# First attention of a four-stage kernel: VectorE's small steps moved ahead of the row maxima, statistics split in parts, two idle banks used for the first batches, and one all-engine barrier left out

## The chip, the cores and the metric

The kernel runs on one core of a Trainium2 chip. The metric is the device time of one execution in microseconds (us), lower is better. The kernel before took 1908.39 us (median of 3 runs, 1903.99 to 1915.61). The profile below is of another execution, which took 1909.73 us with a span of 1907.9 us.

## The reference

The input is x, 16 batches x 256 rows x 256 (4096 rows in all), and a context of the same shape. Four stages follow each other, each adding to x:

```
x = x + xattn0(layernorm(x), ctx)      # the stage that is changed
x = x + ffn0(layernorm(x))             # 8 experts, top 2
x = x + xattn1(layernorm(x), ctx)
x = x + ffn1(layernorm(x))

def xattn0(q, kv, Wq, Wkv, Wc):        # per batch: 256 queries, 256 context rows
    qp = q @ Wq.T
    idx = argmax(qp @ kv.T, axis=-1)   # best context row of each query
    mk, mv = split(kv[idx] @ Wkv.T)    # 16 + 16 columns
    logits = heads(qp) @ mk.T / 4      # 16 heads of 16 columns, 256 x 256 each
    return merge(softmax(logits) @ mv) @ Wc.T
```

## The kernel before

Everything is written as five instruction streams, one for each engine (TensorE, VectorE, ScalarE, GpSimd, and SyncE, which issues most DMAs). Streams meet only through semaphores, and each stream runs strictly in the order written. `Waits.wait_ge` issues a wait once and drops those already passed.

**First attention** (`pe_l0`, `dve_l0`, `act_l0`, `pool_l0`, `sp_l0`). The work is cut into 128 units u (batch u//8, two heads each) and runs over slots i = 0 to 147; g = i//8 is the batch that is scored, r = i%8 the place in it. In slot i TensorE computes the scores of unit i (`scores`, L426), VectorE takes their row maxima (`maxima`, L578, two reductions of 128x512). Fourteen slots later (LAG) TensorE computes the transposed scores with the maxima subtracted (`scores_turned`, L438), ScalarE takes the exponential (`weights`, L673), and every second slot TensorE multiplies by the values (`values`, L450) and ScalarE takes them out (`values_out`, L679). Scores of units rotate over three banks: those of slot u+1 need the first reduction of slot u to be done.

The other steps of a batch hang on a value of r:

- Entry of batch g+2, all in bank MB: r=1 `turn_x` (L477), r=2 `x_out` (L707, ScalarE), r=3 `queries` (L485), r=4 `queries_high` (L713, ScalarE) and `queries_low` (L595, VectorE), r=7 `matches` (L497); then at r=0 of the next batch `best` (L602, L606: the argmax on VectorE) and `memories` (L777: GpSimd gathers the chosen context rows).
- Keys of batch g+1: r=5 `turn_keys` (L505) and `context` of g+2 (L460), r=6 `context_out` (L693, L695) and `keys_high` (L720) on ScalarE, `keys_low` (L613) on VectorE. `matches` at r=7 waits for `keys_low`, since both use MB.
- Exit of batch g-3, all in bank MA: r=3 and r=5 `turn_values` (L512), r=4 and r=6 `divide` (L619, L621, VectorE), r=7 `turn_packed` (L519), r=0 `packed_out` (L725, ScalarE), r=1 `result` (L526), r=2 `result_add` (L627, VectorE), r=3 `stats_out` (mean, variance and a first guess of 1/sqrt, L118 to L133).
- `stats_x` at r=5 of batches 0, 4 and 8: the same statistics for 8 row tiles of x at once, L118 x8 to L133. Newton's steps for 1/sqrt run on GpSimd (`newton_pool`, 14 small operations).

In a slot VectorE did `maxima` first and then what hangs on r; ScalarE did `weights` first. Slots 128 to 147 have no scores; TensorE runs `kv_tile` there (L359, L365: keys and values of the second attention) and VectorE copies the result (L402), again first in its slot. The last batches leave at slots 139 to 147.

**Prologue.** The entries of batches 0 and 1 run before slot 0, both in MB, so one after the other: `best(1)` comes ahead of slot 0. VectorE starts when three transfers have landed (4 row tiles, a weight and the identity).

**Barrier.** `phase_end` (L163 to L167) follows on each engine: a drain, an increment of one semaphore, and a wait until all five have arrived. Then come `pe_route` and its fellows, where VectorE normalises all rows (L159 into XNF) and TensorE transposes them (L953), computes router logits (L962) and one `kv_tile` per step.

Of the kernel before, what the change touches and what calls it, by code (L numbers as in the profile page):

```python
# [56 lines left out]
def build(nc, A, OUT):  # L57
# [57 lines left out]
    def stats_dve(e, w, k, t0, n, mv, r, src, twice=False):  # L115
        v, u, r = LTMP[:, k % 2 * 2, 0:n], LTMP[:, k % 2 * 2 + 1, 0:n], r[:, t0:t0 + n]
        for t in range(t0, t0 + n):
            i = e.bn_stats(ST[:, t, :], src(t))  # L118
        i.then_inc(s_st, 1)
# [15 lines left out]
    def newton_pool(e, w, k, t0, n, r):  # L135
# [24 lines left out]


    s_end = sem("phase_end")

    def phase_end(e, w, n):
        e.drain().then_inc(s_end, 1)
        w.wait_ge(s_end, 5 * n)
# [98 lines left out]
    d_cst, d_w0_w1, d_ws_wr_wc1 = sem("d_cst"), sem("d_w0_w1"), sem("d_ws_wr_wc1")  # L265
    d_x_wf2_out = [sem(f"d_x_wf2_out{i}") for i in range(4)]
    d_ct = [sem(f"d_ct{i}") for i in range(2)]
    d_qw, d_nm, d_x0_wkv_id = sem("d_qw"), sem("d_nm"), sem("d_x0_wkv_id")
# [5 lines left out]
    s_mh, s_wo, s_spl, s_ms = sem("keys0"), sem("outmm0"), sem("ctxsplit"), sem("memsets")  # L274
# [22 lines left out]
    use_a = {}  # L297
    use_b = {n: x for x, n in enumerate((("kv", 0), ("kv", 1), ("xt", 0), ("q", 0), ("am", 0), ("xt", 1), ("q", 1), ("am", 1)))}
    stat0, split_at, nsplit = {"first": 0, ("ln", 0): 1}, {0: 0, 1: 2}, 4
    for i in range(SLOTS0):  # L300
# [4 lines left out]
        for at, n, b in ((1, "xt", g + 2), (3, "q", g + 2), (5, "kv", g + 2), (7, "am", g + 2)):  # L305
            if r == at and is_batch(b) and (n, b) not in use_b:
                use_b[n, b] = len(use_b)
        if i in STAT_AT:
            stat0["o", STAT_AT[i]] = len(stat0)
        if r == 5 and g % 4 == 0 and g < 12:  # L310
            stat0["ln", g // 4 + 1] = len(stat0)
# [106 lines left out]
    def pe_l0(e, w):  # L418
# [35 lines left out]
        def context(b):  # L454
            w.wait_ge(d_x0_wkv_id, 48)
            w.wait_ge(d_ct[b % 2], 16 * (b // 2 + 1))
            w.wait_ge(s_mb, use_b["kv", b])
            for jt in range(2):
                for cc in range(2):
                    i = e.matmul(MB[:, 256 + jt * 32:288 + jt * 32], CT[b % 2][:, cc, jt * 128:jt * 128 + 128], WKV[:, cc, :],  # L460
                                 start=(cc == 0), stop=(cc == 1))
# [8 lines left out]
        def turn_x(b):  # L470
            w.wait_ge(d_x0_wkv_id, 48)
            w.wait_ge(s_xn, b + 1)
            w.wait_ge(s_mb, use_b["xt", b])
            w.wait_ge(s_mh, 3 if b == 2 else 0)
            for cc in range(2):
                for lt in range(2):
                    i = e.transpose(MB[:, cc * 256 + lt * 128:cc * 256 + lt * 128 + 128], XN[:, lt, cc * 128:cc * 128 + 128], ident)  # L477
            i.then_inc(s_xt, 1)

        def queries(b):  # L480
            w.wait_ge(d_w0_w1, 16)
            w.wait_ge(s_mb, use_b["q", b])
            for ec in range(2):
                for cc in range(2):
                    i = e.matmul(MB[:, ec * 256:ec * 256 + 256], WQ[:, cc, ec * 128:ec * 128 + 128], XNT[:, cc, :],  # L485
# [3 lines left out]
        def matches(b):  # L489
            q, c = (QH, QL), [CHL[b % 2][j][:, :].rearrange("p (a b) -> p a b", a=2) for j in range(2)]  # L490
            w.wait_ge(s_spl, split_at[b] + 2)
            w.wait_ge(s_mb, use_b["am", b])
# [1813 lines left out]
```

## Time and profile before

| what | value |
|---|---|
| runs | 1903.99, 1908.39, 1915.61 us |
| profiled execution | 1909.73 us, span 1907.9 us |
| TensorE busy | 1720.9 us, 90% |
| VectorE busy | 1284.1 us, 67% |
| ScalarE busy | 1136.5 us, 60% |
| GpSimd busy | 822.8 us, 43% |
| mean granted TensorE clock | 0.947 |
| first attention with its prologue | 0 to about 445 us |

A line of the page's table of slices shows the busy share of an engine in tenths for each fortieth of the span; the clock line shows the granted TensorE clock in the same way. TensorE's busy time is modelled, since matmuls are pipelined; its idle gaps are therefore more telling than its share.

### The profile page before, as it was taken

The page shows a single profiled execution, that of the slowest core. Times are in us where ns is not written, and L with a number is a line of the kernel's source. Part 1 is how long each engine was busy: PE and PEld are TensorE (multiplying, and loading weights), DVE is VectorE, ACT ScalarE, POOL GpSimd, SP SyncE. Part 2 cuts the span into 40 slices and gives each one's busy share as a digit, 9 for nine tenths or more (in the row PEclk, how much of TensorE's full clock was granted, in tenths as well). Part 3 has the DMA queues.
Part 4 walks back from the last instruction along what each step waited for, and adds up shares of the span by engine and source line. Part 5 has one row for each costly group of instructions (what it writes and reads, how often), then busy time and mean ns, then how long its engine had stood idle before and what let it go on. Part 6 is the DMA issues. An engine that isn't in the chain of part 4 may idle for free.

```text
span 1907.9 us, 41070 instructions
## 1 busy us (share of the span) xinstructions
PE 1720.9 (90%) x15760; PEld 1451.1 (76%) x15760; DVE 1284.1 (67%) x2756; ACT 1136.5 (60%) x2882; POOL 822.8 (43%) x1306
## 2 busy tenths in 40 slices
PE   5789898887999999999999879999999999987648
PEld 3566666666989999999999768788888888866523
DVE  3677887643532888888888386777777777677321
ACT  1356565532336777777777477777777777744210
POOL 3233432111011333333331387888888887654000
PEclk8789999998999999999999999999999999999766
DMA  6754465234786666666676722222222321112699
GB/s 180 202 124 104 107 123 116 61 116 166 263 281 215 246 246 246 243 232 234 244 245 239 234 73 86 71 62 68 90 68 62 92 65 57 43 48 91 233 366 328
DMA packets 140163, 303.81 MB, mean 159 GB/s; under 512 B 14080, under 2 KB 82944, under 8 KB 124736
## 3 DMA queue, kind: packets, MB, share of 16 engines
q1 hardware_dynamic: 116032, 188.68, 32.3%
q0 software_dynamic: 19584, 108.31, 16.8%
q10 hardware_dynamic: 4352, 4.20, 0.6%
q8 instruction: 125, 2.05, 0.4%
q14 instruction: 70, 0.57, 0.1%
HBM read 210.44 MB, written 90.44 MB: 158 GB/s over the span
## 4 chain that ended last, share of the span: by engine, by line
PE 71%; DVE 12%; DMA 5%; issue 5%; POOL 4%; ACT 2%; SPq 1%; POOLq 0%; DVEq 0%; ACTq 0%
PE ps L1230 11%; PE ps L1216 11%; PE ps L1812 5%; PE ps L359 5%; PE ps L223 4%; PE ps L1843 4%; PE ps L1798 4%; PE ps L1832 4%; PE ps L365 3%; DVE NM L578 2%; PE ps L426 2%; DMA rp_scratch<-RP 2%; PE ps L497 2%; PE ps L526 2%; POOL P L213 2%
## 5 line engine op out<-in xcount | busy, mean ns | idle before, releaser
L200 ACT ACTIVATE P<-ps,NM 128x256 f32<-128x256 f32 x512 | 236.2, 481 | 127.5 <-DVE NM L189 127.5
L213 POOL TENSOR_TENSOR P<-P,RS 128x1024 f32<-128x1024 f32 x128 | 242.9, 1903 | 73.7 <-DVE RS L207 73.3
L1216 PE MATMUL ps<-XRP,W1P 128*128 128x256 f32 x1872 | 226.8, 281 | 3.3 <-DVE W1P L1299 3.3
L1216 PEld LDWEIGHTS ps<-XRP,W1P 128*128 128x128 f32 x1872 | 220.1, 190 | 3.6 <-DVE W1P L1299 3.6
L1230 PE MATMUL ps<-W2P,HP 128*128 128x256 f32 x1872 | 221.5, 277 | 0.0
L673 ACT ACTIVATE PT<-ps 128x512 f32<-128x512 f32 x256 | 140.7, 611 | 132.5 <-PE ps L438 132.5
L1230 PEld LDWEIGHTS ps<-W2P,HP 128*128 128x128 f32 x1872 | 218.0, 188 | 0.0
L578 DVE TENSOR_REDUCE NM<-ps 128x2 f32<-128x512 f32 x256 | 164.3, 684 | 64.1 <-PE ps L426 63.9
L189 DVE TENSOR_REDUCE NM<-ps 128x2 f32<-128x512 f32 x256 | 164.6, 684 | 5.6 <-PE ps L1798 4.1
L1150 POOL DMA_INDIRECT WE<-in_we,WIX x39 | 44.2, 1135 | 278.5 <-DVE W1P L1299 209.2
L1259 ACT ACTIVATE HF<-ps,WE 128x256 f32<-128x256 f32 x312 | 129.0, 465 | 43.3 <-PE ps L1216 43.3
L1931 DVE CAST OT<-ps 128x256 fp32r<-128x256 f32 x128 | 54.3, 424 | 141.1 <-PE ps L1812 140.2
L1798 PEld LDWEIGHTS ps<-K,Q 64*128 64x128 f32 x1536 | 100.8, 189 | 59.5 <-issue 42.4
L230 ACT ACTIVATE PT<-ps 128x512 f32<-128x512 f32 x256 | 140.7, 616 | 1.5 <-PE ps L223 1.5
L1812 PE MATMUL ps<-PT,V 128*64 128x256 f32 x1024 | 138.9, 392 | 1.1 <-DVE OT L1933 1.1
L223 PE MATMUL ps<-CST,P 128*128 128x128 f32 x1024 | 133.9, 274 | 3.1 <-ACT PT L230 3.1
L1798 PE MATMUL ps<-K,Q 64*128 64x256 f32 x1536 | 127.3, 299 | 10.3 <-DVE Q L1925 5.4
L1250 ACT ACTIVATE W2P<-WE 128x512 fp32r<-128x512 f32 x156 | 97.3, 624 | 53.9 <-PE ps L1230 53.9
L1146 POOL DMA_INDIRECT XR<-xn_scratch,RIX x78 | 79.4, 1018 | 102.2 <-PE ps L1192 48.1
L223 PEld LDWEIGHTS ps<-CST,P 128*128 128x128 f32 x1024 | 115.1, 141 | 4.6 <-issue 3.9
L1316 DVE TENSOR_TENSOR HP<-HF,HP 128x512 fp32r<-128x512 f32 x156 | 108.0, 692 | 13.2 <-ACT HP L1266 5.7
L1832 PE MATMUL ps<-XNP,W1Q 128*128 128x256 f32 x768 | 110.9, 295 | 4.4 <-POOL XNP L2105 4.4
(219 smaller groups left out, 3710.2 us busy)
## 6 DMA issues: line engine op xcount, KB each, us to landing
KS<-k_scratch SPq DMA_DIRECT2D x64, 256.0 KB, 3.1
V<-v_scratch SPq DMA_DIRECT2D x16, 1024.0 KB, 6.3
rp_scratch<-RP SPq DMA_DIRECT2D x16, 1024.0 KB, 8.8
R<-rp_scratch SPq DMA_DIRECT2D x16, 1024.0 KB, 13.9
k_scratch<-KVM SPq DMA_DIRECT2D x52, 256.0 KB, 4.2
QS<-q_scratch SPq DMA_DIRECT2D x96, 128.0 KB, 4.8
v_scratch<-KVM SPq DMA_DIRECT2D x40, 256.0 KB, 3.0
ys_scratch<-YS SPq DMA_DIRECT2D x39, 256.0 KB, 8.2
```

Of the source, the lines that this page charges most:

```text
L189: e.tensor_reduce(self.NM[:, u % 4, 2 * x:2 * x + 2], PS[SB[n % 3]][:, :].rearrange("p (h j) -> p h j", h=2), AX.X, ALU.max, negate=True). ...
L200: i = e.activation(self.P[u % 4][:, c, :], PS[SB[n % 3]][:, y * 256:y * 256 + 256], ACT.Exp, bias=self.NM[:, u % 4, c:c + 1], accum_out=se ...
L213: e.tensor_tensor(p, p, self.RS[:, u % 4, :].unsqueeze(2).to_broadcast([128, 4, 256]), ALU.mult).then_inc(self.s_pn, 1)
L223: i = e.transpose(PS[TB[h]][:, c0:c0 + 128], self.P[u % 4][:, c, jt * 128:jt * 128 + 128], ident)
L230: e.activation(self.PT[u % 4][h][:, :], PS[TB[h]][:, :], ACT.Copy).then_inc(self.s_tv, 1)
L578: e.tensor_reduce(NM0[b % 2][:, :, 8 * h + p], PS[SB[(2 * u + h) % 3]][:, :].rearrange("p (l j) -> p l j", l=2), AX.X, ALU.max, negate=Tru ...
L673: e.activation(PT0[u % 4][h][:, :], PS[TB[h]][:, :], ACT.Exp).then_inc(s_ex0, 1)
L1216: m = e.matmul(PS[p][:, hh * 256:hh * 256 + 256], W1P[i % 2][wi][:, cc * 1024 + hc * 128:cc * 1024 + hc * 128 + 128], XRP[i % 2][xi][:, cc ...
L1230: m = e.matmul(PS[4 + k][:, s * 256:s * 256 + 256], HP[k][hi][:, hc, s * 128:s * 128 + 128], W2P[k][wi][:, hc * 256:hc * 256 + 256], start ...
L1798: m = e.matmul(PS[SB[(2 * u + h) % 3]][:, lt * 256:lt * 256 + 256], Q1[i][64 * h:64 * h + 64, p, lt * 128:lt * 128 + 128], K1[j][64 * h:64 ...
L1812: m = e.matmul(PS[OB][64 * h:64 * h + 64, 0:256], V1[b % 2][:, jt, (2 * p + h) * 64:(2 * p + h) * 64 + 64], a1.PT[u % 4][h][:, jt * 256:jt ...
L1832: m = e.matmul(QB[:, j * 256:j * 256 + 256], W1Q[wi][:, cc, c0:c0 + 128], XNP[b % 2][xi][:, cc, :], start=(cc == 0 and x == 0), stop=(cc = ...
```

## The change

Six edits, all but one in the first attention:

1. On VectorE `divide` and `result_add` stand ahead of the slot's `maxima` (or copy), `keys_low` behind them.
2. On ScalarE `x_out`, `queries_high`, `context_out`, `keys_high` and `packed_out` stand ahead of the slot's `weights`.
3. `stats_x` is cut into four parts, at r = 1, 3, 5, 7 of the same batches; the first three take 2 tiles each, the last 2 tiles and the rest of the work.
4. In the prologue batch 1 uses bank MA (`entry`), its context and that of batch 0 the banks PS[3] and PS[4] (`context_bank`). `best(1)` moves into slot 0. The order is written anew.
5. The first transfer brings 2 row tiles and not 4, with a semaphore of its own; Newton's steps for them run on VectorE (`newton`, the old `newton_pool` under another name).
6. `phase_end` is gone. SyncE waits for the last `result` before it loads the router's weights.

```diff
+        def stats_x(c, part):
             w.wait_ge(d_x_wf2_out[c], 16)
-            stats_dve(e, w, stat0["ln", c], 8 * c, 8, MV, RSTD, lambda t: X[:, t, :])
+            if part < 3:
+                stats_rows(e, 8 * c + 2 * part, 2, lambda t: X[:, t, :])
+            else:
+                stats_dve(e, w, stat0["ln", c], 8 * c, 8, MV, RSTD, lambda t: X[:, t, :], before=6)
...
-        w.wait_ge(d_x0_wkv_id, 48)
-        stats_dve(e, w, stat0["first"], 0, 4, MV, RSTD, lambda t: X[:, t, :])
+        w.wait_ge(d_x0, 16)
+        stats_dve(e, w, stat0["first"], 0, 2, MV, RSTD, lambda t: X[:, t, :])
+        newton(e, w, stat0["first"], 0, 2, RSTD)
         norms(0)
         w.wait_ge(d_x_wf2_out[0], 16)
-        stats_dve(e, w, stat0["ln", 0], 4, 4, MV, RSTD, lambda t: X[:, t, :])
+        stats_dve(e, w, stat0["ln", 0], 2, 6, MV, RSTD, lambda t: X[:, t, :])
+        queries_low(0)
         norms(1)
-        queries_low(0)
         best(0)
         queries_low(1)
-        best(1)
         keys_low(0)
-        w.wait_ge(d_cst, 32)
+        w.wait_ge(d_cst_wc, 32)
         for i in range(SLOTS0):
             g, r = i // 8, i % 8
-            if i < U:
-                maxima(i)
-            else:
-                tile_out_dve(e, w, i - U)
-            if r == 6 and is_batch(g + 1):
-                keys_low(g + 1)
             if i in DIV0:
                 divide(DIV0[i], 0)
             if i in DIV1:
                 divide(DIV1[i], 1)
             if i in ADD_AT:
                 result_add(ADD_AT[i])
+            if i < U:
+                maxima(i)
+            else:
+                tile_out_dve(e, w, i - U)
             if i in STAT_AT:
                 stats_out(STAT_AT[i])
-            if r == 0 and g and is_batch(g + 1):
+            if r == 0 and is_batch(g + 1):
                 best(g + 1)
             elif r == 4 and is_batch(g + 2):
                 queries_low(g + 2)
-            elif r == 5 and g % 4 == 0 and g < 12:
-                stats_x(g // 4 + 1)
+            elif r == 6 and is_batch(g + 1):
+                keys_low(g + 1)
+            elif r % 2 and g % 4 == 0 and g < 12:
+                stats_x(g // 4 + 1, r // 2)
...
         context_out(0)
-        context_out(1)
         x_out(0)
         queries_high(0)
+        context_out(1)
         x_out(1)
...
-            if 0 <= i - LAG < U:
-                weights(i - LAG)
             if i in PACK_AT:
                 packed_out(PACK_AT[i])
-            if r == 1 and is_batch(g - 1):
-                max_out(g - 1)
-            elif r == 2 and is_batch(g + 2):
+            if r == 2 and is_batch(g + 2):
                 x_out(g + 2)
-            elif r == 3 and is_batch(g + 3):
-                norms(g + 3)
             elif r == 4 and is_batch(g + 2):
                 queries_high(g + 2)
             elif r == 6 and is_batch(g + 1):
                 if is_batch(g + 2):
                     context_out(g + 2)
                 keys_high(g + 1)
+            if 0 <= i - LAG < U:
+                weights(i - LAG)
+            if r == 1 and is_batch(g - 1):
+                max_out(g - 1)
+            elif r == 3 and is_batch(g + 3):
+                norms(g + 3)
...
-            phase_end(e, w, 1)
```

(The last line stands on all five engines.) VectorE's stream in slots r = 4 to 7 of one batch was this; L578 are the maxima (two for each slot), L619 and L621 a division, L595 `queries_low`, L613 `keys_low`:

```order
L578 TENSOR_REDUCE NM_85<-ps 128x2 x2
L619 RECIPROCAL RS_97<-ps 128x16
L621 TENSOR_TENSOR ON<-ps,RS_97 128x256
L595 SCALAR_TENSOR_TENSOR QL<-ps,QH 128x512
L578 TENSOR_REDUCE NM_85<-ps 128x2 x4
L613 TENSOR_TENSOR MKS_78<-ps,MKS_78 16x256 x2
L619 RECIPROCAL RS_97<-ps 128x16
L621 TENSOR_TENSOR ON<-ps,RS_97 128x256
L578 TENSOR_REDUCE NM_85<-ps 128x2 x2
```

Now it is this (L592 the maxima, L636 and L638 the division, L612 `queries_low`, L630 `keys_low`):

```order
L636 RECIPROCAL RS_97<-ps 128x16
L638 TENSOR_TENSOR ON<-ps,RS_97 128x256
L592 TENSOR_REDUCE NM_85<-ps 128x2 x2
L612 SCALAR_TENSOR_TENSOR QL<-ps,QH 128x512
L592 TENSOR_REDUCE NM_85<-ps 128x2 x2
L636 RECIPROCAL RS_97<-ps 128x16
L638 TENSOR_TENSOR ON<-ps,RS_97 128x256
L592 TENSOR_REDUCE NM_85<-ps 128x2 x2
L630 TENSOR_TENSOR MKS_78<-ps,MKS_78 16x256 x2
L592 TENSOR_REDUCE NM_85<-ps 128x2 x2
```

Both divisions stand ahead of their slot's maxima, and the second one is no longer behind `keys_low`.

ScalarE's stream in slot r = 6 of a batch was this; PT are the exponentials, CKV `context_out`, MKS `keys_high`, OT `values_out`:

```order
L673 ACTIVATE PT_87<-ps 128x512
L673 ACTIVATE PT_88<-ps 128x512
L693 ACTIVATE CKV<-ps 128x128 x2
L695 ACTIVATE CKV<-ps 128x2x16
L720 ACTIVATE MKS_76<-ps,CST 128x256
L679 ACTIVATE OT_96<-ps 128x256
```

Now it is this:

```order
L710 ACTIVATE CKV<-ps 128x128 x2
L712 ACTIVATE CKV<-ps 128x2x16
L737 ACTIVATE MKS_76<-ps,CST 128x256
L690 ACTIVATE PT_87<-ps 128x512
L690 ACTIVATE PT_88<-ps 128x512
L696 ACTIVATE OT_96<-ps 128x256
```

The four operations on context and keys stand ahead of the two exponentials. Behind the change VectorE's slots 0 to 3 of batch 0 read so (L592 the maxima, L619 and L623 `best(1)`, L117 parts of the statistics of x):

```order
L592 TENSOR_REDUCE NM_84<-ps 128x2 x2
L619 MAX MX<-ps 128x8 x2
L623 MAX_INDEX MI<-MX,ps 128x8 x2
L592 TENSOR_REDUCE NM_84<-ps 128x2 x2
L117 BN_STATS ST<-X 128x6 x2
L592 TENSOR_REDUCE NM_84<-ps 128x2 x4
L117 BN_STATS ST<-X 128x6 x2
```

The argmax of batch 1 and the first two parts of the statistics lie between maxima that stood in a row before.

## Rows read from the trace of the kernel before

**Rows 1.** Stretches of the core's time; columns: length, busy us (count) of engines, clock, DMA

```profile
core 0: us, PE busy (x) PEld busy (x) DVE busy (x) ACT busy (x) POOL busy (x), PEclk, DMA share, GB/s
...
178.67:199.19 20.52, 18.29 (x186) 13.28 (x185) 16.42 (x39) 12.93 (x30) 8.41 (x21) 1.00 0.62 126
...
219.70:243.77 24.07, 19.65 (x186) 14.57 (x185) 20.08 (x58) 13.04 (x30) 11.21 (x35) 0.93 0.46 102
...
284.80:306.75 21.95, 19.72 (x186) 14.14 (x185) 16.26 (x39) 13.14 (x30) 6.58 (x19) 0.92 0.54 113
```

**Rows 2.** What TensorE waited for, 36 to 375 us: total, times, longest

```profile
PE ps L519 <- DVE ON L621: 22.4, 12, 2.0
PE ps L426 <- DVE NM L578: 15.4, 12, 3.5
```

**Rows 3.** A regular batch in order of time: start, busy us, what, [idle before]

```profile
178.50 0.98 PE L460 MATMUL ps<-WKV,CT 128*128 128x32 f32 x8
...
179.94 1.29 DVE L578 TENSOR_REDUCE NM<-ps 128x2 f32<-128x512 f32 x2 [0.64 <-PE ps L426]
...
180.19 1.08 ACT L673 ACTIVATE PT<-ps 128x512 f32<-128x512 f32 x2 [1.55 <-PE ps L438]
...
181.55 0.60 ACT L720 ACTIVATE MKS<-ps,CST 128x256 fp32r<-128x256 f32 x1
...
182.18 0.88 DVE L613 TENSOR_TENSOR MKS<-ps,MKS 16x256 fp32r<-16x256 f32 x2 [0.95 <-ACT MKS L720]
...
183.86 0.66 PE L519 MATMUL ps<-CST,ON 128*128 128x128 f32 x4 [2.03 <-DVE ON L621]
...
188.29 2.00 PE L526 MATMUL ps<-WC,ONT 128*128 128x256 f32 x8
...
192.50 0.68 DVE L627 TENSOR_TENSOR X<-X,ps 128x512 f32<-128x512 f32 x1
...
196.11 1.29 DVE L578 TENSOR_REDUCE NM<-ps 128x2 f32<-128x512 f32 x2
...
197.22 0.50 PE L426 MATMUL ps<-MKS,QS 48*128 48x256 f32 x4
```

**Rows 4.** The statistics of 8 tiles in batch 0, order of time

```profile
49.17 2.70 DVE L118 BATCH_NORM_STATS2 ST<-X 128x6 f32<-128x256 f32 x8
...
53.82 0.79 PE L426 MATMUL ps<-MKS,QS 48*128 48x256 f32 x4 [3.49 <-DVE NM L578]
```

**Rows 5.** A stretch of 2 us, columns as in rows 1

```profile
292.00:294.00 2.00, 2.00 (x18) 1.32 (x19) 0.76 (x2) 0.33 (x1) 0.00 (x0) 0.50 0.00 1
```

**Rows 6.** Who waited for whom, 350 to 447 us: total, times, longest

```profile
PE ps L519 <- DVE ON L621: 4.4, 3, 1.6
...
PE ps L512 <- DVE ON L621: 3.3, 3, 1.4
...
PE ps L512 <- DVE X L627: 1.5, 1, 1.5
```

**Rows 7.** The end of the stage and the barrier, order of time

```profile
439.04 0.17 DVE L133 TENSOR_SCALAR RSTD<-LTMP 128x2 int32<-128x2 int32 x1
...
445.71 6.55 DVE L159 TENSOR_SCALAR XNF<-X,MV,RSTD 128x256 f32<-128x256 f32 x20 [6.50 <-POOLq L165]
...
446.59 1.09 PE L953 MATMUL ps<-CST,XNF 128*128 128x128 f32 x4 [10.39 <-DVE XNF L159]
```

**Rows 8.** The prologue and first slots in order of time; last, L834's DMA landing

```profile
11.81 0.74 DVE L159 TENSOR_SCALAR XNa<-X,MV,RSTD 128x256 f32<-128x256 f32 x2 [3.40 <-POOL RSTD L146]
...
23.99 1.16 POOL L777 DMA_INDIRECT MVK<-ckv_scratch,MI  x1 [3.25 <-DVE MI L606]
...
31.64 0.83 SPq L831 DMA_DIRECT2D ctx_scratch<-CHL  x2
...
34.70 0.74 SPq L834 DMA_DIRECT2D X<-in_x  x1
...
40.19 1.29 DVE L578 TENSOR_REDUCE NM<-ps 128x2 f32<-128x512 f32 x2 [0.48 <-PE ps L426]
...
DMA to landing us min/median/max: 9.8/9.8/9.8
```

More of the change, by code:

```diff
@@ L113, in build, with stats_rows, stats_dve @@
     s_st, s_nw = sem("ln_guess"), sem("ln_newton")
-    def stats_dve(e, w, k, t0, n, mv, r, src, twice=False):
-        v, u, r = LTMP[:, k % 2 * 2, 0:n], LTMP[:, k % 2 * 2 + 1, 0:n], r[:, t0:t0 + n]
+    def stats_rows(e, t0, n, src):
         for t in range(t0, t0 + n):
             i = e.bn_stats(ST[:, t, :], src(t))
-        i.then_inc(s_st, 1)
+        return i
+    def stats_dve(e, w, k, t0, n, mv, r, src, twice=False, before=0):
+        v, u, r = LTMP[:, k % 2 * 2, 0:n], LTMP[:, k % 2 * 2 + 1, 0:n], r[:, t0:t0 + n]
+        stats_rows(e, t0 + before, n - before, src).then_inc(s_st, 1)
         w.wait_ge(s_st, 5 * k + 1)
@@ L295, in is_batch, with entry, entry_free, entry_done @@
         return 0 <= b < 16
-    use_a = {}
-    use_b = {n: x for x, n in enumerate((("kv", 0), ("kv", 1), ("xt", 0), ("q", 0), ("am", 0), ("xt", 1), ("q", 1), ("am", 1)))}
+    def entry(b):
+        return MA if b == 1 else MB
+    def entry_free(w, n, b):
+        if b == 1:
+            w.wait_ge(s_ma, use_a[n, 1])
+        else:
+            w.wait_ge(s_mb, use_b[n, b])
+    def entry_done(w, n, b):
+        if b == 1:
+            w.wait_ge(s_ma, use_a[n, 1] + 1)
+        else:
+            w.wait_ge(s_mb, use_b[n, b] + 1)
+    def context_bank(b):
+        return PS[TB[b]] if b < 2 else MB
+    use_a = {("xt", 1): 0, ("q", 1): 1, ("am", 1): 2}
+    use_b = {n: x for x, n in enumerate((("xt", 0), ("q", 0), ("am", 0)))}
     stat0, split_at, nsplit = {"first": 0, ("ln", 0): 1}, {0: 0, 1: 2}, 4
@@ L305, in build @@
         for at, n, b in ((1, "xt", g + 2), (3, "q", g + 2), (5, "kv", g + 2), (7, "am", g + 2)):
-            if r == at and is_batch(b) and (n, b) not in use_b:
+            if r == at and is_batch(b):
                 use_b[n, b] = len(use_b)
@@ L309, in build @@
             stat0["o", STAT_AT[i]] = len(stat0)
-        if r == 5 and g % 4 == 0 and g < 12:
+        if r == 7 and g % 4 == 0 and g < 12:
             stat0["ln", g // 4 + 1] = len(stat0)
@@ L530, in pe_l0 @@
         context(0)
-        context(1)
         turn_x(0)
         queries(0)
+        context(1)
         matches(0)
@@ L536, in pe_l0 @@
         queries(1)
+        turn_keys(0)
         matches(1)
-        turn_keys(0)
         for i in range(SLOTS0):
@@ L581, in norms @@
         def norms(b):
-            w.wait_ge(s_nw, newton_done(stat0["first"]))
+            w.wait_ge(s_nw, newton_done(stat0["ln", 0] if b else stat0["first"]))
             w.wait_ge(s_xt, b)
@@ L778, in memories @@
                                      in_offset=bass.IndirectOffsetOnAxis(ap=MI[:, lt, 0:1], axis=0)).then_inc(d_gk[b % 2], 16)
-        e.memset(CKV[:, :, :], 0.0).then_inc(s_ms, 1)
-        w.wait_ge(s_ms, 1)
-        e.memset(CKV[:, :, 144:145], 1.0).then_inc(s_ms, 1)
-        newton_pool(e, w, stat0["first"], 0, 4, RSTD)
+        e.memset(CKV[:, :, :], 0.0).then_inc(s_ms_ck, 1)
+        w.wait_ge(s_ms_ck, 1)
+        e.memset(CKV[:, :, 144:145], 1.0).then_inc(s_ms_ck, 1)
         split(0)
-        newton_pool(e, w, stat0["ln", 0], 4, 4, RSTD)
+        newton(e, w, stat0["ln", 0], 2, 6, RSTD)
         split(1)
```

109 lines of the change are left out of this document (53 added, 56 removed).

## The prediction

> **What bounds the kernel now.** I read the page first: TensorE is busy 90% of the span, so a gain must come from its gaps. Then the stretches between one batch's `context` and the next. A regular batch of the first attention takes 20.52 us, of which TensorE works 18.29 [rows 1], so 2.23 us are a gap; VectorE works 16.42 and ScalarE 12.93. Third, the list of who waited for whom: nearly all of the gap is one wait, `turn_packed` (L519) for the second division, 22.4 us in 12 waits [rows 2]. The timeline shows how it arises [rows 3]: the context matmuls end at 179.48 (178.50 + 0.98), yet ScalarE first does two exponentials (180.19), then CKV, and only at 181.55 the keys (L720); VectorE stands 0.95 us for them, does `keys_low` (182.18 to 183.06) and the division, and TensorE starts L519 at 183.86 after 2.03 us of nothing. The division's own input had long been there; it stood behind `keys_low` only by order. Two more gaps belong to this change. In three batches VectorE does the statistics of 8 tiles in one piece and TensorE waits 3.49 us for maxima [rows 4]; such a batch takes 24.07 us [rows 1]. And at the end of the stage TensorE waits 10.39 us from its last tile to L953 [rows 7].
>
> **The clock in these gaps.** After the same L519 gap two of the regular batches ran matmuls at a granted clock of 0.50 [rows 5], the lower of the two levels (1.2 GHz), and took 21.95 us [rows 1] (the next one alike) where their neighbours took 20.5. The engine had done nothing for 2.03 us just before the clock fell.
>
> **The change part by part.** The sum is made against the profiled execution, 1909.73 us (span 1907.9 and 1.8 around it), which lies 1.3 us above the median of the runs.
>
> *Divisions first, keys first.* In slot r=6 ScalarE can now start CKV at 179.5, not at 181.16; CKV and keys took 0.99 us together, so the keys stand at 180.5 instead of 182.15. VectorE does the division in the 0.64 us in which it stood before the maxima of 179.94 [rows 3]; maxima end near 181.3, `keys_low` near 182.2. L519 finds its input, `matches` waits for nothing more. The 22.4 us go. What is late next: the two exponentials begin at 180.5 instead of 180.19 and end near 181.6, while TensorE wants their banks at 181.33: 0.27 us per batch. The first division of a batch now stands between the statistics and the maxima of 196.11 and pushes them 0.5 us (the division takes 0.64; the addition, also moved, gives part back); TensorE's next scores come 0.74 us after a start of maxima wherever the trace has them waiting, so 197.35 against 197.22: 0.13 us. Thirteen batches x 0.40 = 5.2. Net **-17.2**. Bounds: -22.4 if neither is seen, and -6 if handing over between the engines costs a full 0.7 + 0.53 us once per batch. The addition (L627) ahead of the maxima costs nothing as long as L526, which ends at 190.29, is done before VectorE would start on its own, and that is near 190.5; the maxima before and after it were 0.8 us apart. `packed_out`, `x_out` and `queries_high` fall in gaps of ScalarE, which works 12.93 of 20.52 us [rows 1]; cover gone, each would cost the 0.60 us that such an operation takes (L720 in [rows 3]).
>
> *The clock dips behind those gaps.* Two batches gave 1.43 and 1.54, and the last scored batch, where after an idle 1.61 us the matmuls of 353 to 360 us ran at half clock, about 3. If the gaps go, so do these: up to -6, at least 0; I take **-5**. The Trainium skill, TensorE: Matmul & The Clock Gate, Part 1, says that activity releases the throttle and idling brings it back; by it the dips vanish with the idle stretches. This trace agrees in direction (clock 0.50 only behind a gap), but nine of the twelve L519 gaps brought no dip, so I don't take the rule as a switch.
>
> *Statistics in parts.* VectorE's chain through such a batch gets no shorter: from slot 0 to slot 10 I add up maxima, best, addition, statistics, divisions and the 4.3 us of parts to 25.7 us with the two handovers, against 23.2 for TensorE's. So these batches become bound by VectorE and exceed a regular one by 2.5 us and not by 3.55 (24.07 - 20.52). With the half-clock matmuls behind the long gap **-3** for batches 4 and 8 (0 to -6).
>
> *Prologue.* VectorE starts after one transfer of half the size and does Newton's steps itself, some 14 steps of 0.2 us; I put the first normalisation at 8.2 instead of 11.81 [rows 8] and, the rest of the chain being the same matmuls and outputs, the gather of batch 0 at 19.9 instead of 23.99. Batch 1's entry lies beside it in bank MA. Scores could start 6 us earlier. But SyncE waits for that gather (31.64) before it stores the split context, and only behind that, at 34.70, it asks for the next 8 row tiles, which land 9.8 us later, at 44.5 [rows 8]. Statistics needed them in slot 5 (49.17 [rows 4]); the first part now needs them in slot 1. Moved up by 4.1 us they land at 40.4, VectorE stands there with the maxima of slot 2 behind it, and these start near 41.1, where they start at 40.19 now. So the prologue's gain is all given back, with `best(1)` hidden in that wait. What is left is the hole of 3.49 us in slot 5, now spread: **-2.4** (bounds +1 and -8, the latter if the rows land as soon as they are wanted). In batches 1 and 2 `matches` waited about 1 us for `keys_low`, which now comes sooner: **-1.5**.
>
> *Tail, slots 128 to 147.* TensorE waits there for divisions and an addition that stand behind a copy which itself needs TensorE's tile of that slot: 4.4 - 1.6 (the one at 352 us is counted above) + 3.3 + 1.5 = 7.6 us [rows 6]. Ahead of the copy they run beside the tile. **-7**.
>
> *Barrier.* VectorE's last statistic ends at 439.2 and its first XNF starts at 445.71 [rows 7]: 6.5 us. Nothing in `dve_route` needs the other engines at once: the first Newton results are hundreds of us old, the last are needed only by the last of 32 normalisations, 20 of which take 6.55 us [rows 7]. The last copy and addition change places, 0.6 more. **-7** (bounds -4, if the loss of cover shows in a bank or a DMA, and -9 with a warmer clock at L953).
>
> *Beyond 447 us* nothing is changed. TensorE is bound there by itself and starts that much earlier; one wait for stores near 530 us moves along. I price it at nothing; cover gone, it is a few us.
>
> Sum: -17.2 - 5 - 3 - 2.4 - 1.5 - 7 - 7 = -43.1, so 1909.7 - 43.1 = **1866.6 us**.
>
> **The rivals.**
>
> *VectorE becomes the bound.* With 16.42 us of work and a dozen waits in 18.6 it has 12% left. If maxima late by half a us make TensorE wait in several slots, a batch takes 19.5: 11 us less gain, and small gaps keep some dips (5 us more): 1882. For it: 15.4 us of waits for maxima already [rows 2]. Against it: the tight slots (even for VectorE, odd for TensorE) alternate.
>
> *First in line is the wrong place (slower).* A division or addition at the head holds the maxima if its input is late. If the three moved steps each expose the matmuls they wait for (L526 2.0, L512 0.66 twice) and their own time (0.68 + 2 x 0.64), 5.3 us per batch come in for 2.0 that go: 13 x 3.3 = 43 us more, the dips stay, and with 21 us from elsewhere the time is 1909.7 + 43 - 21 = 1932. It decides when L526 ends later than VectorE finishes slot 1; the rows have 0.2 us to spare there before VectorE idles, and 1.0 before it costs anything. The same page of the Trainium skill (Architectural detail) calls ScalarE's and VectorE's queues strict FIFO; that rule speaks against putting waiting steps first, and by it alone the time would be this rival's. The row agrees with it: VectorE stood 0.95 us for keys with a ready division behind.
>
> *The rows are there in time.* If the tiles of x land 5 us sooner than I put it, the prologue keeps its gain: 1866.6 - 5.5 = 1861.
>
> *The clock stays up throughout.* All dips of 36 to 447 us vanish, also those behind the statistics and at 447: 6 to 8 us more, 1859.
>
> *The barrier does less than it says*: another wait takes its place, 1872.
>
> **How the numbers follow.** Chances: forecast 0.52, VectorE as bound 0.18, rows in time 0.08, clock up 0.10, barrier replaced 0.05, several of these losses together (near 1890 and above, still not slower) 0.04, slower 0.03. The likeliest case alone spans 1860 to 1875. Taking in the VectorE and the clock rival with the bounds of the terms (-6 instead of -17 for the first, -8 for the prologue) the range is 1853 to 1887. Beyond 1% (19 us, about what a measurement of this kernel can tell) the line is at 1889: faster 0.90, within 0.07, slower 0.03.
>
> **What would show it.** A regular batch from `context` to `context` of 18.4 to 18.9 us; no L519 wait over 0.3 us; a small new wait of L438 for the exponentials in r=6; VectorE idle for 4 to 7 us in slot 1 of batch 0 until a transfer of x lands; the maxima of slot 2 no earlier than 40 us; statistics batches near 21 us; XNF within 0.1 us of the last L136; the part behind it as long as before. I am wrong if regular batches stay above 19.3, if L526 and the addition show up as VectorE's longest wait, or if the stages behind the first attention change their length by more than 3 us.

## The result, and the profile after

| what | before | after |
|---|---|---|
| median of the comparison | 1907.38 us | 1855.94 us (1849.57 to 1860.65, 4 runs) |
| ratio | | 0.9729, interval 0.9697 to 0.9762 |
| the same two once more, in a later measurement | 1906.21 us | 1863.11 us (1860.92 to 1867.99, 6 runs), 0.9774, interval 0.975 to 0.9798 |
| profiled execution, span | 1907.9 us | 1847.8 us; the second one 1861.6 us |
| L953 / L972, the end of the stage | 446.6 us | 394.9 us; the second one 404.9 us |

The forecast was 1866.6 us, that is 43.1 less; measured are 51.4 less and, the second time, 43.1 less. The direction, the size and most of the places were right. The two medians of one kernel lie 7 us apart, though the intervals of their ratios overlap, and the two profiles differ by 10 us at the end of the stage. Where these 10 us lie became the question of the study. Lines moved by up to 19: L519 of before is L533 now, L426 is L440, L438 is L452, L578 is L592, L720 is L737, L953 is L972.

A stretch runs from `context` to the next `context` and is named by the batch in whose slot r = 5 it begins, so that the first one is batch 0. These are stretches of the changed kernel, with the columns of [rows 1]: batch 4 with statistics, a regular one of the early half (GpSimd splits a weight in it), and one of the later half:

```profile
core 0: us, PE busy (x) PEld busy (x) DVE busy (x) ACT busy (x) POOL busy (x), PEclk, DMA share, GB/s
...
125.48:145.30 19.82, 18.43 (x185) 13.32 (x184) 19.09 (x53) 13.72 (x31) 9.94 (x29) 1.00 0.53 119
...
163.98:182.57 18.59, 18.24 (x185) 13.31 (x184) 16.65 (x38) 13.73 (x31) 8.34 (x20) 1.00 0.62 133
...
239.81:257.96 18.15, 18.15 (x186) 13.32 (x184) 16.22 (x38) 13.72 (x31) 6.56 (x18) 1.00 0.64 137
```

Against 20.52 and 24.07 [rows 1] the gaps are nearly gone: in the later half TensorE is busy 18.15 of 18.15. The waits of 100 to 330 us (total, times, longest) no longer have the line that led [rows 2], L519 for a division:

```profile
PE ps L440 <- DVE NM L592: 8.1, 11, 1.4
...
PEld ps L452 <- ACT PT L690: 1.3, 6, 0.4
...
DVE X L644 <- PE ps L540: 0.9, 1, 0.9
```

PEld is TensorE's loading of weights, which overlaps its matmuls; no matmul of L452 stood idle for the exponentials there.

And the same place as [rows 3], a batch in order of time. The division (L636, L638) stands ahead of the maxima of 165.43, the keys (L737) stand 1.42 us after the start of the context matmuls and not 3.05, and L533 follows L452 with no idle time in brackets:

```profile
163.98 0.98 PE L474 MATMUL ps<-WKV,CT 128*128 128x32 f32 x8
164.71 0.24 DVE L636 RECIPROCAL RS<-ps 128x16 f32<-128x16 f32 x1
...
164.98 0.42 DVE L638 TENSOR_TENSOR ON<-ps,RS 128x256 f32<-128x256 f32 x1
...
165.40 0.58 ACT L737 ACTIVATE MKS<-ps,CST 128x256 fp32r<-128x256 f32 x1
165.43 1.29 DVE L592 TENSOR_REDUCE NM<-ps 128x2 f32<-128x512 f32 x2
...
166.75 0.88 DVE L630 TENSOR_TENSOR MKS<-ps,MKS 16x256 fp32r<-16x256 f32 x2
...
167.44 0.66 PE L533 MATMUL ps<-CST,ON 128*128 128x128 f32 x4
```

The prologue, as in [rows 8], ends with the transfer of x issued 2.9 us sooner, VectorE idle until it lands, and the maxima of slot 2 where they were before:

```profile
6.22 1.11 DVE L149 TENSOR_TENSOR RSTD<-RSTD,LTMP 128x2 f32<-128x2 f32 x1
...
9.10 0.73 DVE L162 TENSOR_SCALAR XNa<-X,MV,RSTD 128x256 f32<-128x256 f32 x2
...
20.66 1.17 POOL L794 DMA_INDIRECT MVK<-ckv_scratch,MI  x1 [0.48 <-DVE MI L623]
...
28.86 0.81 SPq L850 DMA_DIRECT2D ctx_scratch<-CHL  x2
...
31.78 0.70 SPq L853 DMA_DIRECT2D X<-in_x  x1
...
39.71 0.75 DVE L117 BATCH_NORM_STATS2 ST<-X 128x6 f32<-128x256 f32 x2 [2.66 <-DMA X<-in_x]
40.38 1.27 DVE L592 TENSOR_REDUCE NM<-ps 128x2 f32<-128x512 f32 x2
```

The end of the stage, as in [rows 7]: XNF directly behind the last statistic, and TensorE idle for 2.97 us, not 10.39:

```profile
394.06 0.17 DVE L136 TENSOR_SCALAR RSTD<-LTMP 128x2 int32<-128x2 int32 x1
394.13 8.15 DVE L162 TENSOR_SCALAR XNF<-X,MV,RSTD 128x256 f32<-128x256 f32 x25
...
394.92 0.98 PE L972 MATMUL ps<-CST,XNF 128*128 128x128 f32 x4 [2.97 <-DVE XNF L162]
```

From L972 to the end of the span nothing is changed: 1461.3 us before, 1452.9 and 1456.7 in the two profiles of after, and 1454.8 to 1463.5 in those of eleven variants. That part scatters by some 10 us, so the experiments below are read by the start of L972 as well as by their medians.

The stage itself, from the first `context` of a slot (batch 0) to the last, before and in the two profiles of after:

```profile
48.45:328.64 280.19, 240.59 (x2217) 175.69 (x2216) 214.74 (x505) 156.94 (x364) 99.84 (x247) 0.91 0.57 128
```

```profile
48.85:294.26 245.41, 230.55 (x2216) 168.29 (x2216) 214.32 (x501) 165.30 (x364) 99.47 (x246) 0.96 0.62 146
```

```profile
49.41:302.42 253.01, 235.82 (x2217) 172.06 (x2216) 215.80 (x501) 165.27 (x364) 99.98 (x246) 0.93 0.60 142
```

TensorE's idle part (length less busy time) fell from 39.6 us to 14.9 and 17.2. Its busy part, for the same matmuls, fell by 10.0 and 4.8 us, mostly by the higher granted clock (a regular batch at 1.00 has 18.29 us before and 18.15 to 18.24 after). So the gaps account for most of the gain in both profiles, and the clock for two thirds of the difference between them.

### The profile page after: what moved, and what is told of

It is laid out like the page before. It is cut to its first block, busy times and chain, and to the rows that moved or that the text cites. A ratio compares the mean times of both kernels' runs of the same rounds, so it can differ in the third digit from the quotient of the medians.

```text
span 1847.8 us, 41058 instructions
## 1 busy us (share of the span) xinstructions
PE 1707.3 (92%) x15760; PEld 1443.4 (78%) x15760; DVE 1286.2 (70%) x2770; ACT 1145.3 (62%) x2882; POOL 821.8 (44%) x1292
## 3 DMA queue, kind: packets, MB, share of 16 engines
q0 software_dynamic: 19584, 108.31, 17.2%
## 4 chain that ended last, share of the span: by engine, by line
PE 74%; DVE 9%; DMA 7%; POOL 4%; issue 4%; ACT 1%; SPq 1%; DVEq 0%; POOLq 0%; ACTq 0%
PE ps L1250 12%; PE ps L1236 11%; PE ps L1832 5%; PE ps L373 5%; PE ps L219 4%; PE ps L1863 4%; PE ps L1818 4%; PE ps L1852 4%; PE ps L379 3%; PE ps L464 3%; PE ps L440 2%; DMA R<-rp_scratch 2%; DVE NM L592 2%; DMA rp_scratch<-RP 2%; POOL P L209 2%
## 5 line engine op out<-in xcount | busy, mean ns | idle before, releaser
L592 DVE TENSOR_REDUCE NM<-ps 128x2 f32<-128x512 f32 x256 | 164.3, 684 | 35.9 <-PE ps L440 35.1
```

The costliest lines, as they stand in the source:

```text
L592: e.tensor_reduce(NM0[b % 2][:, :, 8 * h + p], PS[SB[(2 * u + h) % 3]][:, :].rearrange("p (l j) -> p l j", l=2), AX.X, ALU.max, negate=Tru ...
```

## The experiments

**The barrier back.**

```diff
 # after each engine's part of the first attention; the definition of phase_end returns too
+            phase_end(e, w, 1)
```

> The changed kernel with the barrier of all engines put back behind the first attention. Theory (a barrier costs what GpSimd still has to do, Newton's steps of the last batch, plus its drain): the first XNF comes 6.8 us later than in the changed kernel (VectorE's last statistic at 394.2, Newton to about 398, drain 2.95), and the time rises by the same, about 6.8 us over the changed kernel's 1855.9. Rival (the next stage would have waited for these Newton results anyway): less than 1 us.

Measured: 1871.24 us, ratio to before 0.9814 (interval 0.9785 to 0.9843). From the last `context` to L978 (L972 of the changed kernel) it took 109.02 us, against 100.66 and 102.45 in the two profiles of after: 6.6 to 8.4 us. The wait for GpSimd's part of the barrier is back:

```profile
406.62 0.17 DVE L136 TENSOR_SCALAR RSTD<-LTMP 128x2 int32<-128x2 int32 x1
...
413.29 2.99 DVE L162 TENSOR_SCALAR XNF<-X,MV,RSTD 128x256 f32<-128x256 f32 x9 [6.50 <-POOLq L168]
```

The price of the barrier is as forecast, and it is made of GpSimd: its Newton steps go on until 410.54, and the barrier releases VectorE at 413.29; the 2.75 us between are put down to GpSimd's drain, which no row shows by itself. The median rose by more than the forecast 6.8 (15.3 us against the first median of after, 8.1 against the second), and this profile showed two pairs of batches near 22 us that the first profile of after had not. This was the first sign of what comes below.

**VectorE's old order in a slot.**

In short form, not the code's own lines:

```diff
-            (divide, divide, result_add) then maxima(i); keys_low at the end
+            maxima(i); keys_low; then (divide, divide, result_add)
```

> The changed kernel with VectorE's old order inside a slot (maxima first, the keys' low part, then divisions and addition); ScalarE's new order stays. Theory (the division's place is what TensorE waits for): in slot 6 the division ends behind maxima and keys, L533 starts about 0.9 us later in each of 13 batches, and the tail gets its 6.5 us of waits back: 18 us slower than the changed kernel, near 1874. Rival (late keys on ScalarE were the cause, and they are early now): only the tail, +6.5 us.

Measured: 1875.91 us, 0.9839 (0.9809 to 0.9869), near the theory's 1874; stage end (start of L972) at 417.2. The wait for the division is back, half as long per batch as in [rows 2], since ScalarE's keys still come first (100 to 345 us):

```profile
PE ps L533 <- DVE ON L638: 10.3, 11, 1.1
```

**ScalarE's old order in a slot.**

In short form:

```diff
-            packed_out, x_out, queries_high, context_out, keys_high, then weights(i - LAG)
+            weights(i - LAG), then the others
```

> The changed kernel with ScalarE's old order inside a slot (exponentials first); VectorE's new order stays. Theory: keys come 1.3 us later, the matches (L511) then wait for them about 0.4 us per batch, since L533 no longer does: +5 us on the changed kernel, near 1861. Rival (ScalarE's order carried the gain of a regular batch): +1.5 us per batch, +20 us, near 1876.

Measured: 1877.54 us, 0.9857 (0.9828 to 0.9887); stage end at 418.2. The rival was right: ScalarE's order is worth as much as VectorE's. With late keys it is now `matches` and the maxima that wait (100 to 345 us), and regular batches take 19.31 to 19.5:

```profile
PE ps L511 <- DVE MKS L630: 7.7, 10, 0.8
PE ps L440 <- DVE NM L592: 7.3, 8, 1.7
```

**Both orders alone, in the kernel before.** The edits of the two experiments above, made the other way round in the kernel before; barrier, prologue and statistics as before.

> The kernel before with only the new orders inside a slot on VectorE and ScalarE (edits 1 and 2). Theory (the orders carry the regular batches, their clock dips and the tail): regular batches of 18.2 to 18.7 us, -37 us against the kernel before, near 1871. Rival (the prediction's own terms for these edits, 17.2 + 5 + 7): -29 us, near 1878, regular batches of 18.6 or more.

Measured: 1873.24 us, 0.9841 (0.981 to 0.9871); stage end at 414.2, 32.4 us earlier than before. Regular batches take 18.15 to 18.6, those with statistics in one piece 24.14 and 23.34. The batches came as the theory had them; the time, 32.2 us less, lies between it and the rival and nearer to the rival's 29. Some two thirds of the gain are the two orders; with either old order back the kernel took 13 to 22 us more than the two medians of after, so neither alone holds most of the gain: the keys need ScalarE's order to come early, the division needs VectorE's.

**The statistics in one piece.**

```diff
-            elif r % 2 and g % 4 == 0 and g < 12:
-                stats_x(g // 4 + 1, r // 2)
+            elif r == 5 and g % 4 == 0 and g < 12:
+                stats_x(g // 4 + 1)
```

> The changed kernel with the statistics of 8 row tiles in one piece at r=5 again. Theory (the hole of over 3 us on TensorE costs its own time and the half-clock matmuls behind it): batches 4 and 8 take 23 to 24 us and not 19.8, batch 0 some 2 us more: +9 us, near 1865. Rival (VectorE's chain has the same length either way, as my sum had it): +1 to +2 us.

Measured: 1863.33 us, 0.9775 (0.9745 to 0.9804); stage end at 404.4. Batches 4 and 8 take 24.19 and 23.58, as the theory had it, but those behind them 18.69 and 18.17. Against the first median of the changed kernel that is 7.4 us more; against the second measurement of the changed kernel (0.9774) nothing is lost: one batch of 24.2 and one of 18.7 are as long as two of 21.6 and 21.1.

**The rows of x first.** `rows_in(1)` issued right behind the first loads and not at 31.78.

> The changed kernel with the second load of row tiles (1 MB) issued right behind the first loads and not behind the gather of batch 0. Theory: VectorE's wait of 2.66 us for rows in slot 1 of batch 0 goes, the first L972 comes 2.5 us earlier than 394.9. Rival (the early megabyte delays the tiles 2 to 7, the second context and the gather): no gain or up to 3 us lost.

Measured: 1859.22 us, 0.9743 (0.9714 to 0.9772). The wait in slot 1 is gone and the first `context` comes at 45.76, not 48.85; but the stage ended at 408.4, with batches 4, 5, 8 and 9 at 21.97, 22.16, 21.97 and 21.6. Batches 1 and 2 took 20.5 and 19.76, where TensorE waited 1.81 us for gathered context rows at 86.68; the kernel with the statistics in one piece, whose rows come as before, has such a wait of 2.07 at 88.77, so this is no sign that the early megabyte delays the gather. The forecast gain cannot be seen in the time.

**GpSimd's weight split three slots later.** In slot 2 of a batch GpSimd splits the context (L779, L781) and then a weight (L785, L787); the weight's part is moved to slot 5.

> The changed kernel with GpSimd's split of a piece of the second attention's weights moved from r=2 to r=5, away from VectorE's statistics. Theory (VectorE's small TENSOR_SCALAR on SBUF cannot run while GpSimd does a two-operand operation: L132 took 0.60 us beside L787 and 0.17 elsewhere): batches 4 to 11 go from 18.6 to 18.2 us, first L972 3 us earlier. Rival (these batches are longer for other work, such as the load of these weights): no change.

Measured: 1855.37 us, 0.973 (0.9708 to 0.9751). Regular batches of the early half take 18.17 and not 18.59, so 0.4 us per batch was indeed lost there; batches 4, 5 and 8 took 20.51, 19.58 and 20.22. The stage ended at 397.5, not 3 us before 394.9, and the median is that of the first measurement of the changed kernel (0.9729): by itself the move shows no gain in the time.

**The gather of batch 1 ahead of slot 0** (`matches(1)` before `turn_keys(0)`, `best(1)` before `keys_low(0)`, on top of the early rows).

> As e6, and in the prologue the matches of batch 1 stand ahead of the turn of batch 0's keys on TensorE, and the argmax of batch 1 ahead of batch 0's low keys on VectorE. Theory: 2.7 us of half-clock matmuls move into the 7.1 us in which TensorE waits for the gather, and the argmax leaves slot 0: scores start 0.4 us sooner and slot 1 about 2 us sooner than in e6; first L972 at 390 to 390.5. Rival (the argmax waits for the same gather and only pushes the keys): as e6, 392.4.

Measured: 1860.77 us, 0.9774 (0.9745 to 0.9804); first `context` at 44.38, stage end at 395.9 where 390 to 390.5 was forecast, and again no gain in the time. Batches 4 and 8 took 21.97 and 21.99, with no step held for longer than 0.79 us (the held steps are explained below). Half-clock matmuls follow here on gaps of 0.93 and 0.99 us at the end of the batch before:

```profile
121.95:143.92 21.97, 21.05 (x186) 15.40 (x185) 19.27 (x53) 13.86 (x31) 10.77 (x32) 0.84 0.53 112
```

**The changed kernel once more.**

> The changed kernel itself, once more. Five earlier runs of its variants (barrier back, rows early) showed batch periods near 22 us behind the statistics of batches 4 and 8, where the first profile of the changed kernel showed 18.7 to 19.9. Theory: these slow batches come and go between executions of one and the same kernel. Then this profile may show them or not, the other batches stay at 18.1 to 18.7 us, the router starts at 395 to 405 us, and the median is 1856 +- 3 us. Rival: they belong to the variants (their edits cause them); then this profile has the same periods as the first within 0.1 us and the router at 395.

Measured: 1863.11 us, 0.9774 (0.975 to 0.9798), 4 us above the forecast range. The stage ends at 404.9. The same code now has the slow pairs (batches 4 and 5, 8 and 9), so they are not peculiar to the variants:

```profile
125.23:146.83 21.60, 18.89 (x185) 13.94 (x184) 20.03 (x54) 13.86 (x31) 11.03 (x34) 0.97 0.52 115
146.83:167.88 21.05, 20.59 (x184) 14.96 (x184) 16.28 (x37) 13.64 (x30) 8.23 (x20) 0.86 0.46 110
167.88:186.48 18.60, 18.23 (x185) 13.31 (x184) 16.68 (x38) 13.78 (x31) 8.38 (x20) 1.00 0.64 138
...
205.72:226.97 21.25, 18.52 (x186) 13.39 (x184) 19.67 (x53) 13.54 (x31) 10.77 (x32) 1.00 0.54 117
226.97:247.93 20.96, 20.96 (x186) 15.38 (x185) 16.24 (x38) 14.03 (x31) 6.60 (x18) 0.84 0.40 109
```

These two pairs are 8.4 us longer than in the first profile, of 10.0 us by which the stage ends later. The timeline of the slot r = 3 of batch 5, where `stats_out` stands between the statistics of batch 4 and the next division, shows where the two part. First profile of the changed kernel:

```profile
140.44 1.27 POOL L781 TENSOR_TENSOR CHL<-CT,CHL 128x512 fp32r<-128x512 f32 x1
...
141.34 0.40 DVE L132 TENSOR_SCALAR LTMP<-MV 128x2 f32<-128x2 f32 x1
...
141.77 0.52 DVE L134 TENSOR_SCALAR LTMP<-LTMP 128x2 int32<-128x2 int32 x1
...
142.34 1.29 POOL L787 TENSOR_TENSOR W1K<-WS,W1K 128x512 fp32r<-128x512 f32 x1
...
143.77 0.50 PE L440 MATMUL ps<-MKS,QS 48*128 48x256 f32 x4 [0.50 <-DVE NM L592]
```

Its second profile:

```profile
142.13 1.28 POOL L787 TENSOR_TENSOR W1K<-WS,W1K 128x512 fp32r<-128x512 f32 x1
142.24 1.20 DVE L134 TENSOR_SCALAR LTMP<-LTMP 128x2 int32<-128x2 int32 x1
...
143.84 0.42 DVE L638 TENSOR_TENSOR ON<-ps,RS 128x256 f32<-128x256 f32 x1
144.18 1.28 DVE L592 TENSOR_REDUCE NM<-ps 128x2 f32<-128x512 f32 x2
...
144.92 0.50 PE L440 MATMUL ps<-MKS,QS 48*128 48x256 f32 x4 [1.83 <-DVE NM L592]
```

L134 is a step over 2 values per partition that takes 0.17 us by itself. Here VectorE comes to it 0.11 us after GpSimd has begun its subtraction of 512 values, and it ends with that subtraction (143.44 and 143.41). The division and the maxima stand behind it, TensorE has nothing to do for 1.83 us instead of 0.50, and in the next batch its granted clock is 0.86 and not 1.00: 20.59 us of matmuls where the same matmuls take 18.23. In the first profile VectorE was through with L134 (held 0.52 us, beside the cast before it) 0.05 us before the subtraction began. The Trainium skill, SBUF — State Buffer, section "SBUF: two separate sides", calls the port pair that VectorE and GpSimd share an exclusive lock, held for a whole instruction, for which the loser blocks, where VectorE's instruction is in a 2-port mode or has two inputs in SBUF. The rows agree that L134 waits for the end of GpSimd's instruction; in which mode it runs they do not show. Not every step of VectorE is held: L117 took its usual 0.74 us beside L781.

How far do the other kernels fall in line? A small step of 1.13 to 1.23 us in that slot of batches 5 and 9 stands in the profiles of the barrier (L132, L136), of the early rows (L134), of the second one of after (L134) and of the next two experiments (L134). In all ten places TensorE then idles for 1.69 to 2.07 us and the batch behind has a clock of 0.81 to 0.91. Where the longest such step is 0.8 us or less (first profile of after, match first, all together) the batch behind batch 4 takes 18.6 to 18.7.

But the held step is not the only road to a low clock, and not always one. With VectorE's old order L136 took 1.13 us in both places, and yet the gap was only 0.93 and 0.94 us; batch 5 took its regular 19.56, batch 9 19.84 at a clock of 0.91. With ScalarE's old order the steps took 1.13 and 1.10, the gaps were 1.67 and 1.29, and batches 5 and 9 stayed at a clock of 1.00 (19.51 and 19.33 us). The other way round, half-clock matmuls followed on gaps of 0.59 to 0.99 us without any long step: in the weight split (batch 4 at 0.92, batch 5 at 0.91), in match first (batches 4 and 8 at 0.84) and with ScalarE's old order (batch 8 at 0.85). Gaps of 0.91 and 0.98 us in the first profile of after brought none. So the held step is where the two profiles of the changed kernel part, and the gap and the clock behind it make the 8.4 us. Why VectorE reached these statistics 0.69 us later in the second (L117 at 140.97 and not 140.28) no row shows. When a gap below 1 us lowers the clock stays open, and so does how often the step is held in executions that were not profiled.

**The statistics spread over eight batches.** The first three parts go to slot 5 of batches 1, 2, 3 and of 5, 6, 7; the last part stays in slot 7 of batches 4 and 8.

```diff
+            elif r == 7 and g in (4, 8):
+                stats_x(g // 4 + 1, 3)
+            elif r == 5 and 0 < g < 8 and g % 4:
+                stats_x(g // 4 + 2, g % 4 - 1)
```

> The changed kernel, with the first three parts of the statistics for the second and third later group moved out of batches 4 and 8, one each to slot 5 of batches 1, 2, 3 and 5, 6, 7; only the last part (2 tiles and the small steps) stays in slot 7 of batches 4 and 8. Theory (VectorE's extra work of about 2 us sets the length of these two batches, and the gap that it opens is what the slow batches behind follow from): batches 4 and 8 take 18.3 to 19.0 instead of 19.85, no period of 20 us or more beyond batch 3, router start 2 to 10 us earlier than the unchanged kernel's median, median 1852. Rival (the part in slot 7 with Newton's steps on GpSimd beside it is the costly one, or the slow batches come from elsewhere): periods of 20 to 22 remain at batches 4 and 8, median 1856.

Measured: 1862.47 us, 0.977 (0.9742 to 0.9798), the same as the changed kernel beside it. The theory fell: with 2 us less to do on VectorE in front, batches 4 and 8 still take 21.08 and 20.7, and behind them 20.95 and 19.48. Batches 3 and 4 are each half a us shorter than in the second profile of after (18.69 for 19.18, 21.08 for 21.60); that much can be VectorE's sum of work. L134 is held all the same (1.20 us at 140.93), and with it the gap of 1.83 us and the low clock are there.

**Spread, and the rows early.**

> The same spreading, and the transfer of rows 8 to 15 issued right behind the first loads, so that VectorE does not stand in slot 1. Theory: context(0) 3 us earlier, batches 4 and 8 at most 19 us, so 3 us less than the spread kernel: 1849. Rival: in the rows-early run the earlier transfer ended in slow batches elsewhere and gained nothing; then the early batches take 20 to 22 us again and the median is within 2 us of the spread kernel.

Measured: 1860.53 us, 0.9753 (0.9729 to 0.9777); slow batches as before (21.15, 20.85, 20.7, 20.97), although the first `context` comes 2.3 us sooner. The rival was right in the median, 1.9 us below that of the spread kernel; the early batches took 20.29, 19.56 and 18.3, not 20 to 22.

**All together**: spread, rows early, the gather of batch 1 ahead of slot 0, and the weight split in slot 5.

> Spreading, rows early, best(1) ahead of slot 0 beside the other entry work, and GpSimd's weight split moved to slot 5. Theory: all four gains add: batches 0 to 3 at 18.2 to 21, batches 4 and 8 at most 19, all regular ones at 18.16, router start near 385, median 1846. Rival: VectorE has no slack left at slots 5 and 7 with GpSimd beside it, some batches take 20 and more, router start 392 or later, median 1854.

Measured: 1850.21 us (1845.22 to 1854.7, 6 runs), 0.9706 (0.9681 to 0.9732). On the same chip the changed kernel took 1863.11, and the two intervals do not meet: it beats both kernels, by 12.9 us the changed one. The stage ends at 389.1 us. Both lie between the theory (1846, 385) and the rival (1854, 392). The subtraction of the weight is out of the slot of `stats_out`, and all three small steps take 0.17 (L136 too):

```profile
133.87 1.28 POOL L786 TENSOR_TENSOR CHL<-CT,CHL 128x512 fp32r<-128x512 f32 x1
...
135.71 0.17 DVE L132 TENSOR_SCALAR LTMP<-MV 128x2 f32<-128x2 f32 x1
135.92 0.17 DVE L134 TENSOR_SCALAR LTMP<-LTMP 128x2 int32<-128x2 int32 x1
...
137.57 0.50 PE L440 MATMUL ps<-MKS,QS 48*128 48x256 f32 x4 [0.83 <-DVE NM L592]
```

```profile
119.44:139.10 19.66, 18.34 (x185) 13.35 (x184) 18.05 (x51) 13.53 (x31) 11.24 (x34) 1.00 0.64 133
139.10:157.72 18.62, 18.31 (x185) 13.35 (x184) 16.80 (x40) 13.72 (x31) 8.41 (x20) 1.00 0.51 122
```

The spread kernel with early rows, which differs from this one by the weight split and the order in the prologue, took 1860.53 on that chip; the stage ends 10.3 us earlier here. The first `context` comes 1.7 us earlier, the rest falls in the batches. No run moves the weight split on top of the spread kernel and nothing else, so what share of these 12.9 us is the split's stays open. So does this: batch 9 took 19.49 at a clock of 0.91 here too, behind a gap of only 0.8 us.

## Why the prediction was right, point by point

- **Divisions and keys first, -17.2**: right in its mechanism. The division's input was there, the keys come early, and the wait of L533 is gone from the scored batches. Regular batches fell by 1.9 to 2.35 us, to 18.6 and 18.15, where 18.4 to 18.9 was put. Of the two new waits the one for the exponentials did not come: only weight loads of L452 waited, 1.3 us in six times, and no matmul. The one for maxima, priced at 0.13 us, is 0.3 to 0.45 us in batches of the early half (where L132 is held for 0.60 us) and nothing in the later half. What the step missed is that the two orders are not one term and a remainder: with ScalarE's old order alone the kernel took 14 to 22 us more, with VectorE's 13 to 20 us.
- **Clock dips, -5**: the dips behind the old L519 gaps have gone with them. Two things in the reading were wrong. It counted three such dips among twelve gaps; the gap at 117.03 has one too (the matmuls of 118 to 120 us ran at 0.50), and the statistics batches and batch 2 had others (batch 2: clock 0.83, 18.88 us of matmuls, now 16.07). And new dips come and go behind the statistics, which were not in the sum. In all, busy time fell, mostly by the clock, by 10.0 us in one profile and 4.8 in the other from the first `context` to the last, where about 3 of these 5 were put. That is most of what sets the two profiles apart; of the 7 us between the medians 1863 and 1856 it is the likely cause, not a shown one, since only one execution of each measurement was profiled.
- **Statistics in parts, -3**: the size stands between the two profiles (batches 4 and 8 at 19.8 or at 21.3 to 21.6, "near 21" was put), but the reason given holds only in part. I said that VectorE's sum of work binds such a batch; when 2 us of it were taken out, batches 3 and 4 each became half a us shorter and no more. Without any held step (all together) batch 4 still takes 1.0 us more than a regular one, in gaps of 0.49 and 0.83 us for maxima, which is VectorE's chain. The second profile's batch 4 takes 1.8 us more than the first's: 1.3 us of gap behind the held step, 0.5 by the clock. The kernel with the statistics in one piece took 0.2 and 7.4 us more than the two medians of after, so what the parts are worth is not settled.
- **Prologue, -2.4 and -1.5**: the gain is given back at the transfer of x, as put, but two errors cancelled there, and that was luck. The transfer was issued 2.9 us sooner and not 4.1, and it landed 7.9 us after its issue and not 9.8; 40.4 was put and 39.7 measured. VectorE idled 2.66 us for it, outside the 4 to 7 us that were named as a sign. The other marks are within 1 us (normalisation 9.10 for 8.2, late by L149's 1.11 beside GpSimd; gather 20.66 for 19.9; maxima of slot 2 at 40.38 for 41.1). The first `context` of a slot came 0.4 and 1.0 us later than before and batch 0 took 2.0 and 2.7 us less (23.29 to 21.29 and 20.56), so 1.6 to 1.8 us for the 2.4. Of the waits of `matches` behind the 1.5, the one in batch 1 (1.09 us) went and the one in batch 0 (0.81) stayed. Batches 2 and 3 gave 2.8 us each (20.10 to 17.26, 22.01 to 19.16), in batch 2 all of it by the clock.
- **Tail, -7, and barrier, -7**: from the last `context` to L972 the profiles have 17.3 and 15.5 us less. TensorE's idle part fell by 16.3 and 16.2 of that; 14 and the L519 wait of 1.6 us counted in the first term make 15.6. The barrier alone, put back, cost 6.6 to 8.4. One wait of 1.08 us for a division is left at 386.70.
- **Beyond the stage, 0**: the part behind it is 8.4 and 4.6 us shorter in the two profiles, which is more than the 3 us that were named as a sign of being wrong. Eleven variants with the same code there have 1454.8 to 1463.5 us, so the sign was set below the scatter of that part, and nothing shows an effect of the change.
- **The sum**: that the second measurement gives 43.1 us to the digit is luck. Terms were off by several us, mostly to the low side, and new clock dips took back what they missed; the first measurement of the same code gives 51.4. The upper end of the range, 1887, is 4 us above what the terms named for it add up to (1866.6 + 11.2 + 5 = 1882.8).
- **The rivals**: VectorE as the bound holds for the statistics batches in part, as said, and not for the regular ones; moved steps at the head held nothing (0.9 us in one wait for L540), so the rule of strict order cost nothing here, because their inputs were there. The clock that stays up throughout, 1859, is near to what the first profile shows: 1.00 from 89 us to the last `context`, but 0.64 and 0.82 in batches 0 and 1.

## What to carry to other kernels

In a slot of fixed order, put the steps whose input is long there, and that others wait for, ahead of the large step that itself waits; look at both engines of such a chain, since either one's order alone gave back only a part. When one kernel's profile has batches of two lengths, compare two executions of it and look for the first operation that took another time: here it was one step of 0.17 us that took 1.2 beside GpSimd, and more than half of what it cost came afterwards, in the clock. Taking work off VectorE left the held step and its gap as they were; in the kernel that also moved the neighbour on GpSimd they were gone, though the move by itself, in the kernel as it was, brought no gain that could be measured.

## What the hardware showed

- VectorE's small steps with all operands in SBUF (TENSOR_SCALAR, TENSOR_TENSOR) took 0.40 to 1.23 us instead of 0.16 or 0.17 beside GpSimd's cast or subtraction over 512 values, and ended with it; BATCH_NORM_STATS2 and steps that read PSUM (L638) kept their length.
- Idle stretches of TensorE of 1.69 to 2.07 us behind a held step were followed by a batch at a mean granted clock of 0.81 to 0.91 in ten places (at 0.86 the batch was 2.4 us longer), while one of 1.67 us was followed by 1.00. After stretches of 0.59 to 0.99 us the clock fell in some places (to 0.84 in the batch, twice) and stayed at 1.00 in others.
- Whether the small step is held differs between two executions of the same code: VectorE began L134 0.11 us behind the start of GpSimd's subtraction in one, and had ended it 0.05 us before that start in the other. The medians of the two measurements are 1855.94 and 1863.11 us, against 1907.38 and 1906.21 of the kernel before.
